# Another order of the engines' work in the second pass of a linear-attention and FP4-FFN kernel

## The reference

```python
xn = layernorm(x)
# attention block, 16 heads of 64
Q = elu(xn @ Wq + bq) + 1;  K = elu(xn @ Wk + bk) + 1;  v = xn @ Wv + bv
KV = einsum('bshd,bshm->bhdm', K, v)               # sums over the 2048 rows
Z  = 1 / (einsum('bshd,bhd->bsh', Q, K.sum(1)) + 1e-6)
o  = einsum('bshd,bhdm,bsh->bshm', Q, KV, Z)
x1 = layer_norm(xn + o @ Wo + bo) * g1 + be1
s  = layer_norm(x1 + gelu(x1 @ W1 + b1) @ W2 + b2) * g2 + be2     # 256 -> 1024 -> 256
# gated FFN, 256 -> 704 -> 256, inputs and weights rounded to FP4 in blocks of 16
q(t) = fp4_quant_dequant(t)                        # scale = max|block| / 6
h  = silu(q(xn) @ q(w_gate).T) * (q(xn) @ q(w_up).T)
g  = silu(q(h) @ q(w_down).T)
out = x + s * g
```

## Time and profile before

| | |
|---|---|
| median of 3 runs | 1667.33 us (1667.31 to 1667.33) |
| the execution that was profiled | 1668.97 us |
| its span | 1667.2 us |
| its mean granted TensorE clock | 0.998 of full speed |
| PE busy | 1640.6 us (98%) |
| DVE busy | 1300.8 us (78%) |
| ACT busy | 978.6 us (59%) |
| POOL busy | 784.1 us (47%) |

### The profile page before, as it was taken

How to read it: one execution, slowest core, us unless ns; L and a number is a source line. 1 busy time by engine, 2 the same in 40 slices (tenths; PEclk the granted TensorE clock), 3 DMA queues, 4 the chain that set the end, 5 groups by cost and what they waited for, 6 DMA issues and landing times.

```text
span 1667.2 us, 30550 instructions
## 1 busy us (share of the span) xinstructions
PE 1640.6 (98%) x11105; PEld 1467.2 (88%) x11105; DVE 1300.8 (78%) x2571; ACT 978.6 (59%) x1770; POOL 784.1 (47%) x750
## 2 busy tenths in 40 slices
PE   7999999999999999999999999999999999999997
PEld 6878888888899998989999999989899999999897
DVE  6685664555879797888879897979787887979796
ACT  6665666655464656565655656465656565564644
POOL 4564443434234445444453535444544446353447
PEclk9999999999999999999999999999999999999999
DMA  7322323331300101021010102010101111010100
GB/s 229 122 88 85 102 77 117 109 101 72 117 2 1 52 1 51 3 103 51 2 52 1 51 2 105 2 51 2 51 13 40 65 42 51 1 52 1 52 1 26
DMA packets 69987, 89.36 MB, mean 54 GB/s; under 512 B 8384, under 2 KB 54604, under 8 KB 68815
## 3 DMA queue, kind: packets, MB, share of 16 engines
q1 hardware_dynamic: 69838, 87.42, 16.0%
HBM read 53.30 MB, written 34.10 MB: 52 GB/s over the span
## 4 chain that ended last, share of the span: by engine, by line
PE 69%; DVE 2%; POOL 1%; ACT 0%; issue 0%; POOLq 0%; DVEq 0%
PE QH L81 7%; PE AC L81 7%; PE AC L83 7%; PE AC L82 7%; PE QH L83 7%; PE QH L82 7%; PE GU L81 5%; PE GU L83 5%; PE GU L82 5%; PE TT L821 3%; PE QH L715 2%; PE DN L700 2%; PE DN L81 2%; PE DN L82 2%; PE DN L83 2%; DVE x L1860 1%
## 5 line engine op out<-in xcount | busy, mean ns | idle before, releaser
L1217 ACT ACTIVATE rh<-QH 128x512 fp32r<-128x512 f32 x256 | 149.2, 597 | 82.5 <-DVE QH L1933 77.7
L81 PE MATMUL GU<-wgh,xqh 128*128 128x352 f32 x512 | 169.8, 332 | 0.9 <-DVE hb L1768 0.4
L82 PE MATMUL GU<-wgl,xqh 128*128 128x352 f32 x512 | 165.1, 322 | 0.0
L83 PE MATMUL GU<-wgh,xql 128*128 128x352 f32 x512 | 165.0, 322 | 0.0
L2428 POOL TENSOR_TENSOR hb<-hb,rs_h 128x704 f32<-128x704 f32 x64 | 89.0, 1391 | 158.0 <-DVE rs_h L1775 158.0
L1264 ACT ACTIVATE hb<-GU 128x352 f32<-128x352 f32 x128 | 59.4, 464 | 175.5 <-PE GU L83 173.8
L1948 DVE TENSOR_TENSOR rl<-QH,rh 128x512 fp32r<-128x512 f32 x128 | 86.9, 689 | 87.0 <-ACT rh L1217 85.7
L81 PE MATMUL AC<-Mh,rh 128*128 128x256 f32 x512 | 145.7, 285 | 0.1
L81 PE MATMUL AC<-w2h,rh 128*128 128x256 f32 x512 | 144.5, 282 | 0.0
L82 PE MATMUL AC<-w2l,rh 128*128 128x256 f32 x512 | 142.8, 279 | 0.0
L83 PE MATMUL AC<-w2h,rl 128*128 128x256 f32 x512 | 142.8, 279 | 0.0
(11 more groups left out here) (244 smaller groups left out, 5695.2 us busy)
## 6 DMA issues: line engine op xcount, KB each, us to landing
xa<-in_L_attn_src SPq DMA_DIRECT2D x16, 512.0 KB, 4.2
xt_scratch<-xth SPq DMA_DIRECT2D x32, 256.0 KB, 2.8
xt_scratch<-xtl SPq DMA_DIRECT2D x32, 256.0 KB, 3.0
xb<-in_L_attn_src SPq DMA_DIRECT2D x16, 512.0 KB, 4.2
xnTh<-xt_scratch SPq DMA_DIRECT2D x32, 256.0 KB, 4.7
xnTl<-xt_scratch SPq DMA_DIRECT2D x32, 256.0 KB, 5.4
out<-x SPq DMA_DIRECT2D x15, 512.0 KB, 6.6
m_scratch<-mh SPq DMA_DIRECT2D x16, 256.0 KB, 2.4
```

Of the source, the lines that this page charges most:

```text
L81: e.matmul(outp, lh, rh, start=start, stop=False, skip_group_check=check)
L82: e.matmul(outp, lh, rl, start=False, stop=False, skip_group_check=check)
L83: return e.matmul(outp, ll, rh, start=False, stop=stop, skip_group_check=check)
L1217: e.activation(RH[j % 4][:], src, ACT.Copy).then_inc(S[sem], 1)
```

## The change

The lists of PE, ACT, DVE and POOL are written in another order; SP's is not. The loop now starts at `q_proj(g, 2)` on PE instead of `f_step(g, 3)` and holds one group g; the first group's calls ahead of it and the last group's calls behind it are written out. No helper is changed, and every engine has as many instructions as before (PE 9117 rows of instructions or runs of them, DVE 2121, POOL 754 in both). Behind PE's block the line numbers shift: L1771, L1773, L1775 become L1764, L1766, L1768; L1948 becomes L1941; L2510 becomes L2502; L2526 becomes L2518.

The core of the diff, by engine:

```diff
 # PE, start of the second pass
             q_proj(0, 0)
+            turn_xq(0, 0)
             q_proj(0, 1)
             kv_map(NB - 1, 0)
...
             m_map(NB - 1, 1)
-            turn_xq(0, 0)
             q_proj(0, 4)
 # PE, the loop (before it is written with g + 1 and a + 4 for the same group)
-                turn_h(a + 4, 0)
-                z_spread(g + 1, 7)
-                at_step(g + 1, 4)
-                turn_h(a + 4, 1)
-                at_step(g + 1, 5)
+                z_spread(g, 7)
+                turn_h(a, 0)
+                at_step(g, 4)
+                at_step(g, 5)
+                turn_h(a, 1)
...
-                gate_up(a + 4, 0)
-                turn_h(d, 0)
-                den_sums(g + 1)
+                turn_h(d - 4, 0)
+                gate_up(a, 0)
+                den_sums(g)
...
 # DVE, start of the second pass
+            x_round(0, 0)
             q_elu(0, 0)
-            x_round(0, 0)
             kv_out(NB - 1, 0)
 # DVE, the loop
-                gate_mul(c + 4, 1)
-                h_scale(b + 4)
-                h_lo(a + 4, 1)
-                ln1_add(g + 1, 0)
-                ln1_stats(g + 1, 0)
-                ln1_add(g + 1, 1)
-                ln1_stats(g + 1, 1)
+                h_scale(b)
+                gate_mul(c, 1)
+                ln1_add(g, 0)
+                ln1_stats(g, 0)
+                ln1_add(g, 1)
+                h_lo(a, 1)
+                ln1_stats(g, 1)
...
-                gate_mul(d + 4, 0)
-                h_max(c + 4)
-                gelu_lo(g + 1, 0)
-                gelu_lo(g + 1, 1)
-                h_scale(c + 4)
-                gate_mul(d + 4, 1)
+                gate_mul(d, 0)
+                h_max(c)
+                h_scale(c)
+                gelu_lo(g, 0)
+                gate_mul(d, 1)
+                h_lo(b, 0)
+                gelu_lo(g, 1)
 # DVE, the end
+            h_lo(NT - 2, 0)
+            h_lo(NT - 2, 1)
             h_round(NT - 1)
+            gelu_lo(NG - 1, 7)
             g_mul(NT - 3)
-            gelu_lo(NG - 1, 5)
-            h_lo(NT - 2, 0)
-            gelu_lo(NG - 1, 6)
-            h_lo(NT - 2, 1)
-            gelu_lo(NG - 1, 7)
 # POOL, the loop
-                h_in(b + 4)
-                h_out(b + 4)
-                final_mul(g)
-                final_add(g)
-                h_in(c + 4)
-                h_in(d + 4)
-                h_out(c + 4)
+                h_in(a)
+                x2_affine(g - 1)
+                h_out(a)
+                final_mul(g - 1)
+                final_add(g - 1)
+                ln1_rstd(g, 0)
+                ln1_rstd(g, 1)
+                h_in(b)
+                h_out(b)
                 x1_residual(g)
+                h_in(c)
+                h_out(c)
+                h_in(d)
                 x_in(g + 1, 0)
```

More of the change, by code:

```diff
@@ L950, in _ @@
             f_step(0, 4)
-            turn_h(2, 0)
+            f_step(0, 5)
+            turn_xq(1, 0)
             q_proj(1, 1)
[L953 to L956, removed]
             f_step(0, 6)
[L958 to L967, removed]
@@ L987, in _ @@
[L987 to L1005, removed]
@@ L1006, in _ @@
[L1006 to L1011, removed]
             for g in range(1, NG - 1):
                 a, b, c, d = 4 * g, 4 * g + 1, 4 * g + 2, 4 * g + 3
-                f_step(g, 3)
+                q_proj(g, 2)
+                q_proj(g, 3)
+                f_step(g - 1, 7)
+                q_proj(g, 4)
+                q_proj(g, 5)
+                gate_up(a, 1)
+                q_proj(g, 6)
@@ L1017, in _ @@
+                f_step(g, 3)
                 f_step(g, 4)
-                turn_h(c, 0)
+                f_step(g, 5)
+                turn_xq(g + 1, 0)
                 q_proj(g + 1, 1)
[L1020 to L1023, removed]
                 f_step(g, 6)
[L1025 to L1029, removed]
@@ new lines, in _ @@
+                ln_stats("lnb", g - 1)
+                q_elu(g, 6)
+                q_elu(g, 7)
+                gate_mul(a, 0)
+                h_max(a)
+                den_inverse(g)
+                z_parts(g)
+                gate_mul(b, 0)
+                z_mul(g, 0)
+                z_mul(g, 1)
+                h_lo(d - 4, 0)
+                z_lo(g, 0)
+                h_scale(a)
+                z_lo(g, 1)
+                g_mul(c - 4)
+                h_lo(d - 4, 1)
+                z_mul(g, 2)
@@ L2269, in _ @@
+                gate_mul(d, 1)
+                h_lo(b, 0)
+                gelu_lo(g, 1)
+                gelu_lo(g, 2)
+                h_max(d)
+                h_round(c)
+                gelu_lo(g, 3)
+                gelu_lo(g, 4)
+                x_max(g + 1, 0)
+                h_scale(d)
+                h_lo(b, 1)
+                g_mul(a)
+                x_scale(g + 1, 0)
                 gelu_lo(g, 5)
-                x_max(g + 1, 0)
                 gelu_lo(g, 6)
+                x_round(g + 1, 0)
@@ L2342, in _ @@
[L2342 to L2352 removed]
+            gate_mul(NT - 4, 1)
+            ln_stats("lnb", NG - 2)
+            q_elu(NG - 1, 6)
+            q_elu(NG - 1, 7)
+            gate_mul(NT - 4, 0)
@@ new lines, in _ @@
+            h_max(NT - 4)
+            den_inverse(NG - 1)
+            z_parts(NG - 1)
+            gate_mul(NT - 3, 0)
+            z_mul(NG - 1, 0)
+            z_mul(NG - 1, 1)
+            h_lo(NT - 5, 0)
+            z_lo(NG - 1, 0)
+            h_scale(NT - 4)
+            z_lo(NG - 1, 1)
+            g_mul(NT - 6)
+            h_lo(NT - 5, 1)
+            z_mul(NG - 1, 2)
+            z_mul(NG - 1, 3)
+            gate_mul(NT - 3, 1)
+            z_lo(NG - 1, 2)
+            z_lo(NG - 1, 3)
@@ new lines, in _ @@
+            xq_lo(NG - 1, 1)
+            h_round(NT - 4)
+            z_mul(NG - 1, 4)
+            z_mul(NG - 1, 5)
+            g_mul(NT - 5)
+            z_lo(NG - 1, 4)
+            z_lo(NG - 1, 5)
+            h_max(NT - 3)
+            z_mul(NG - 1, 6)
+            z_mul(NG - 1, 7)
+            h_lo(NT - 4, 0)
+            z_lo(NG - 1, 6)
+            z_lo(NG - 1, 7)
+            h_scale(NT - 3)
+            gate_mul(NT - 2, 1)
+            ln1_add(NG - 1, 0)
+            ln1_stats(NG - 1, 0)
@@ new lines, in _ @@
+            ln1_add(NG - 1, 1)
+            h_lo(NT - 4, 1)
+            ln1_stats(NG - 1, 1)
+            gate_mul(NT - 2, 0)
+            ln1_norm(NG - 1)
+            xT_half(NG - 1, 0, "x1T", "x1Th", "x1Tl")
+            xT_half(NG - 1, 1, "x1T", "x1Th", "x1Tl")
+            h_round(NT - 3)
+            gate_mul(NT - 1, 0)
+            h_max(NT - 2)
+            h_scale(NT - 2)
+            gelu_lo(NG - 1, 0)
+            gate_mul(NT - 1, 1)
+            h_lo(NT - 3, 0)
+            gelu_lo(NG - 1, 1)
```

779 lines of the change are left out of this document (364 added, 415 removed).

## The result

| | before | after |
|---|---|---|
| median | 1667.33 us (4 runs, 1667.31 to 1669.23) | 1732.78 us (4 runs, 1730.97 to 1734.85) |
| the execution that was profiled | 1668.97 us | 1730.97 us |
| its span | 1667.2 us | 1729.2 us |
| its mean granted TensorE clock | 0.998 | 0.986 |

The change makes the kernel slower by 3.9%: the ratio is 1.039, with a 95% interval of 1.0372 to 1.0408. The forecast was 1707.3 us in a range of 1671 to 1718, so the direction is right and the size too small by 25 us.

The account below looks back on a forecast made before the run. PE was taken to set the pace at 77.2 us a group; 33.0 + 4.5 + 1.2 + 1.3 = +40.0 us on the median of 1667.33 gave 1707.3 us, range 1671 to 1718.

Parts of the forecast that it names:

- h_scale beside x1_residual: Steady groups: POOL's x1_residual holds a DVE scaling operation, so PE's h_proj(g,2) stalls 2.20 us; 15 times, 33.0 us.
- Rival 1: Steady groups: DVE scaling and POOL's operation miss each other, so the 33.0 us fall away; 1674.3 us, chance 0.20.
- Rival 3: Steady groups: POOL's second x1_residual operation also holds L1773, 2.3 us more per group; 1742 us, chance 0.08.
- The start: Start of second pass: PE waits at the moved turn_xq(0,0) for POOL's x_out, +4.5 us (bounds 3 and 6).
- the sum of 40.0: Whole kernel: predicted slowdown in us, from 33.0 + 4.5 + 1.2 + 1.3.
- Small moves: Steady group: small order changes and two waits that go, +0.08 us a group, +1.2 us in all.
- The two prices for single waits: Steady group: turn_h(d,0) ahead of gate_up(a,0), +0.22 us; h_lo(a,1) between ln1_add and second ln1_stats, +0.15 us.
- the two waits that were to go: PE, steady group: waits of q_proj behind turn_h, -0.19 us, and at turn_h(a,1), 0.10 us, disappear.
- the two costly moves: Steady group: turn_h(d,0) ahead of gate_up(a,0), +0.22 us, and h_lo(a,1) behind ln1_add, +0.15 us.
- Tail: Last group: h_round(NT-1) behind h_lo(NT-2,1) starts POOL's h_out(NT-1) later, +1.3 us (bounds 0 and 4).

Follow-up runs that it names:

- The filled pause: Changed kernel with 18 more transposes on PE at the end of turn_h(b, 0) of each group: 1720.30 us, ratio 1.0314.

## Why the prediction was right and wrong

**h_scale beside x1_residual** was the term that counts, and its mechanism and size hold: 2.20 us forecast, 2.19 measured, in all 15 groups. Three runs take the stall away in three ways (order on the DVE, order on POOL, layout) and land at 1684.8 to 1691.2 us. Rival 1, that the engines miss each other, did not happen once in 15, though the starts are 0.01 us apart. Rival 3, the second hold of L1766, did not either. Its time of 1742 was nearer to the result than mine, but by luck.

**The step that failed** is "By that rule the sum would be 1.65 us larger (half of 3.3); I leave it out of the sum, since no pause of full idleness shows it here". I put the clock at nothing, and weighed it for the start alone and not for the 15 pauses that I had just forecast, each of 2 us in a PE that otherwise hardly stands. PE's clock fell to the lower level behind 9 of them, at 1.6 us each, and at two pauses at the start, where the 5.0 and 3.3 us at half clock cost some 4. These 18 to 19 us are most of the 22 by which the profiled executions differ from the sum of 40.0. The filled pause shows that it is the pause which does it: 12.5 us back for more work. The page "TensorE: Matmul & The Clock Gate" of the Trainium skill, section "Why this matters for your kernels", says that an idle gap between bursts of matmuls takes the array back to the lower clock. The trace agrees in direction only: the page means longer gaps than these, and here 6 of 15 pauses of 1.95 us passed without it, as did one of 2.14 us at 447.2 in the changed kernel with the other layout of am_h. With the lower clock behind all 15 stalls they would have come to 33.0 + 15 x 1.65 = 57.8 us and the sum to 1732; that this is the measured time would have been luck, since only 9 fell and the other terms were larger than forecast. Why these 9 and not the others was not settled.

**The start** was forecast as a wait of 4.5 us; it was 4.4, and the rest of the 8.9 is the lower clock behind it (5.2 us at 0.51 are 2.6 us), and a second wait, for the denominators (2.1 us where it was 1.3), with its own stretch at 0.50. That "nothing behind wins this back" missed that the clock and a second wait would add to it.

**Small moves.** The two prices for single waits hold (0.22 forecast, 0.22 measured from the z_spread ahead of gate_up(b, 1); 0.15 forecast, 0.10 measured at turn_x1), and the two waits that were to go are gone. But the periods at full clock are 0.26 us longer than before and the stall, where 0.08 was forecast: 0.2 to 0.3 us a group appear in steps that I had not priced, more of z_spread and the down products among them. Undoing the two costly moves brought nothing, as PE then waited longer for ln1_norm and at den_sums: such terms do not add.

**Tail**: 1.3 against 2.0, in the bounds. The last h_out starts 1.5 us later against the group, but POOL is no longer the chain there: PE waits 1.5 us for ACT's high part of h, and the chain that ends last runs through PE's products.

**The range** ended at 1718 because it held no case in which a stall costs more than its own length; rival 3, left out whole, would have widened it for the wrong reason.

## What to carry to other kernels

A wait on the engine that sets the pace costs its length and, if PE stands in it, perhaps its clock: price both, and where a pause of this size is certain, filling it with useless transposes can be worth more than it costs (12.5 us here). When orders of DVE and POOL are moved, look for small one-input SBUF operations that now start beside a long operation of POOL; a change of POOL's order or of the operand's shape takes the hold away, and one of the DVE's order takes it out of PE's way. Undo an order on all engines together: here one list put back alone only moved the wait.

## What the runs showed that I had not expected

- L1764 started at 558.42, 0.01 us behind POOL's L2502 and before L2428 had ended (558.45), in the same way in 15 of 15. With x1_residual moved away it starts as far ahead of the end of L2428 and takes 0.19. So it is the operation that POOL starts 0.01 us ahead which holds it, and 0.01 us was enough for POOL to win each time.
- RECIPROCAL (L1768) took 0.43 us beside L2505, as alone.
- 88 bytes of unused memory in each partition made the kernel before 0.65% slower.
